# Identity products in TensorE's waits of the last batch's chain, and all input rows' products first at the end

## The chip, the cores and the metric

One core of a Trainium2 chip runs the whole program in one launch. The metric is the device time in microseconds; the kernel before was run three times.

## The reference

The inputs are `x` (4, 512, 256), the attention weights, a gate (256, 32) and the weights of 32 experts (96 inner columns each), all in float32. Cut to what matters:

```
qkv    = x @ w_qkv                                   # 16 heads of 16
scores = where(causal, (q / 4) @ k.T, -1e10)
a      = softmax(scores) @ v @ w_out
x      = layernorm(x + a)
w      = softmax(x @ gate); take the 4 largest of 32, scaled to sum 1
for each token and each of its 4 experts e:
    g, u = split(x @ gate_up[e]);  y_e = (u * silu(g)) @ down[e]
x      = layernorm(x + sum over the 4 experts of w_e * y_e)
```

There are 2048 tokens, so 8192 pairs of token and expert. The pairs are sorted by expert into tiles of 128 rows; each expert's last tile is filled up, and 95 tiles are computed.

## The kernel before, in words

**The plan.** `make_plan` writes one list of small units. Each engine walks this list and emits its own part of each unit, so each engine's instructions are in the order of the list, and an instruction that waits holds up all that is behind it on its engine. Semaphores join the engines. PSUM has eight banks of 512 float32 columns: banks 0 and 1 serve the row maxima ("max"), 2 and 3 the scores ("st"), 4 and 5 the products with v ("pv"), 6 and 7 in turn the many small units (the tuple `MISC`).

**The last batch's chain.** For the batch with number `B - 1` = 3 the list ends, after the last score and "pv" units, with: "norm" (transposes of the raw output, L612), "att" (transposes of the normalised one, L621), four "proj" (output projection and router logits, L660; VectorE adds the input and takes the statistics behind each, L1025 to L1034), "fix", "find" and "mark" (VectorE finds the four experts of each token, L1049 to L1074), "place" (TensorE sums the marks, so that each pair gets its row, L670), "slots", "count" (L677), "ends" (L684) and "table" (L708). From the table TensorE and SyncE read at which row each tile begins and which expert it belongs to. The semaphore `max_free` reaches `5 * PAIRS` = 160 once VectorE has read the last row maximum.

**Rows out to memory.** GpSimd scatters every token's row four times into `scratch_slots` (L1300), four batches of 16 scatters each. SyncE's queue holds, in this order: "early" (loads of the first `EARLY` = 17 tiles, L414, which only need the rows of batches 0 to 2), "fill" (32 stores of padding behind each expert's rows, L495), a wait for the padding and for all rows of batch 3 (L496 to L499), and the loads of the other 78 tiles (L414 again, called from L501).

**The experts.** TensorE works in a pipeline of four stages for each tile: transposes (L717), gate and up product (L730), transpose of the hidden rows (L740), down product (L746). This pipeline runs once over the tiles 0 to 16, is drained, and runs once over 17 to 94. ScalarE copies the result to `Y` (L899) and GpSimd scatters it into `scratch_y` (L1307).

**The end.** SyncE waits for all scatters and loads `YL`, sixteen transfers of 512 KB, two for each n of eight (L507). For each n TensorE adds in one bank, with the identity as the stationary operand: the input rows `X` (L778, one matmul) and two of the four experts' rows (L781, two matmuls). GpSimd adds the other two (L1314), VectorE joins both sums (L1229), takes the statistics (L931 to L936) and, for the n before, finishes the scale (`refine`, L941 to L949); ScalarE scales the rows (L803) and SyncE writes the result (L510). `X` is already normalised at that time (the wait on `ln_out`, L772). The kernel before uses bank n % 4, so from n = 4 on it waits for VectorE (L776).

Of the kernel before, what the change touches and what calls it, by code (L numbers as in the profile page):

```python
# [12 lines left out]
B, S, D = 4, 512, 256  # L13
H, HD = 16, 16
NE, FF = 32, 96
NT = B * S // 128
# [5 lines left out]
TILES = B * S * TOPK // 128 + NE - 1  # L22
# [10 lines left out]
PAIRS = 8 * B  # L33
# [144 lines left out]
def build(nc, x, w_qkv, w_out, gate, gup, dwn, out):  # L178
    ctx = ExitStack()
    with ctx:  # L180
# [9 lines left out]
        place = [base]  # L190
# [10 lines left out]
        X = sb("X", [128, NT, D], F32)  # L201
# [8 lines left out]
        idf = sb("idf", [128, 128], F32)  # L210
        idb = sb("idb", [128, 128], BF16)
# [70 lines left out]
        YL = at("YL", [128, NT // 2, 2, TOPK, D], F32)  # L282
        PS = ctx.enter_context(nc.psum_tensor("PS", [128, 8, 512], F32))
# [15 lines left out]
        for u in plan:  # L299
            kinds[u[0]] = kinds.get(u[0], 0) + 1  # L300
            rank[u] = kinds[u[0]]
            if u[0] in MISC:
                n_misc += 1
                k = n_misc % 2
# [16 lines left out]
        max_full, max_free = sem("max_full"), sem("max_free")  # L321
# [13 lines left out]
        gu_full, sg_out, hh_out = sem("gu_full"), sem("sg_out"), sem("hh_out")  # L335
        ht_full, ht_out = sem("ht_full"), sem("ht_out")
        y_full, y_out = sem("y_full"), sem("y_out")
        yk_out = [sem(f"yk_out{r}") for r in range(NY)]
        yl_in = [sem(f"yl_in{a}") for a in range(NT // 2)]
        late_sum, early_sum, x_sum = sem("late_sum"), sem("early_sum"), sem("x_sum")  # L340
# [171 lines left out]

        @block.tensor
        def _(e):
            for u in plan:
                kind, a = u[0], u[1:]
                if kind in MISC:
                    k = 6 + bank[u][0]
                    done = misc_full[bank[u][0]]
                if kind == "xt":  # L520
# [4 lines left out]
                    for q in range(4):  # L525
                        t = e.transpose(PS[:, k, 128 * q:128 * q + 128],
                                        X[:, 4 * b + q, 128 * c:128 * c + 128], idf[:, :])
                    t.then_inc(done, 1)
                elif kind == "qk":
# [3 lines left out]
                    for c in range(2):  # L533
                        e.wait_ge(*free(("xt", b, c)))
                        t = e.matmul(PS[:, k, :], WQ[:, c, 128 * m:128 * m + 128], XT[:, b % 2, c, :],  # L535
                                     start=(c == 0), stop=(c == 1))
                    t.then_inc(done, 1)
                elif kind == "v":
# [4 lines left out]
                    for q in range(2):  # L543
                        t0 = 128 * (2 * half + q)
                        for c in range(2):
                            t = e.matmul(PS[:, k, 256 * q:256 * q + 256], XT[:, b % 2, c, t0:t0 + 128],  # L546
                                         WQ[:, c, 512:768], start=(c == 0), stop=(c == 1))
                    t.then_inc(done, 1)
                elif kind == "max":
                    i, n = a  # L550
                    g, r = i // 4, (i // 4) % RG
# [5 lines left out]
                    for h, qt, c0 in pair_scores(n, 2 * (i % 4), 3, 2, 1):  # L557
                        w = 128 * (qt + 1)
                        e.matmul(PS[:, kk, c0:c0 + w], QS[r][0:96, h, 128 * qt:128 * qt + 128], KS[r][0:96, h, 0:w],  # L559
                                 start=(c0 == 0), stop=False, skip_group_check=True)  # L560
# [10 lines left out]
                elif kind == "st":  # L571
                    p, n = a
                    g, r = p // 4, (p // 4) % RG
# [16 lines left out]
                elif kind == "pv":  # L590
                    g, n = a
# [176 lines left out]
            load_experts(EARLY)  # L768
            experts(EARLY, TILES)

            e.wait_ge(hh_out, TILES)
            e.wait_ge(ln_out, NT)  # L772
            for n in range(NT // 2):
                k = n % 4
                if n >= 4:
                    e.wait_ge(x_sum, n - 3)  # L776
                sums = PS[:, k, :].rearrange("p (q d) -> p q d", q=2)
                e.matmul(sums, idf[:, :], X[:, 2 * n:2 * n + 2, :], start=True, stop=False)  # L778
                e.wait_ge(yl_in[n], 32)
                for r in range(2):  # L780
                    t = e.matmul(sums, idf[:, :], YL[:, n, :, r, :], start=False, stop=(r == 1))  # L781
                t.then_inc(early_sum, 1)

        @block.scalar
# [139 lines left out]
        def _(e):  # L924
# [300 lines left out]
            for t in range(0, NT + 2, 2):  # L1225
                if t < NT:
                    e.wait_ge(early_sum, t // 2 + 1)
                    e.wait_ge(late_sum, t // 2 + 1)
                    e.tensor_tensor(X[:, t:t + 2, :], PS[:, t // 2 % 4, :].rearrange("p (q d) -> p q d", q=2),  # L1229
                                    YL[:, t // 2, :, 2, :], ALU.add).then_inc(x_sum, 1)  # L1230
                    variance(t, x_sum, t // 2 + 1)
                if t:
                    refine(B + t // 2, t - 2, 2)
# [103 lines left out]
```

## Time and profile before

| | us |
|---|---|
| median of three runs | 473.64 |
| lowest and highest run | 470.53, 474.44 |
| time of the execution that was profiled | 470.53 |
| its span, first to last instruction | 468.8 |
| around the span (470.53 - 468.8) | 1.7 |
| PE busy | 401.1 (86%) |
| DVE, ACT, POOL busy | 281.8, 245.8, 244.0 |
| mean granted TensorE clock | 0.954 of full speed |

PE is TensorE, PEld its weight loads, DVE VectorE, ACT ScalarE, POOL GpSimd, SP SyncE (SPq its queue of issued transfers). All starts are in microseconds from the span's first instruction. PEclk is the TensorE clock that was granted, 1.00 being 2.4 GHz and 0.50 being 1.2 GHz. A float32 matmul stands in the records as two. In brackets behind a row is the idle time before it and what ended it.

### The profile page before, as it was taken

How to read it: one execution, taken by the hardware profiler on the slowest of the kernel's cores; microseconds unless marked ns; L12 is line 12 of the kernel's file. 1: busy time of each engine (PE TensorE's matmuls, PEld its weight loads, DVE VectorE, ACT ScalarE, POOL GpSimd, SP SyncE). 2: the span in 40 equal slices, each digit the busy share in tenths (PEclk: the TensorE clock that was granted, in tenths of full speed). 3: DMA queues.
4: the chain of work that ended last, by engine and by line, in shares of the span. 5: the costliest groups of instructions: out<-in, count | busy, mean ns of one | idle time of the engine just before them, and what ended most of it. 6: DMA issues, size and time to landing. Idle time of an engine off the chain costs nothing.

```text
span 468.8 us, 9779 instructions
## 1 busy us (share of the span) xinstructions
PE 401.1 (86%) x2613; PEld 268.1 (57%) x2613; DVE 281.8 (60%) x835; ACT 245.8 (52%) x594; POOL 244.0 (52%) x362
## 2 busy tenths in 40 slices
PE   5755899999988899978988717979999999996692
PEld 2422565455564356544544416859889998984240
DVE  1225774787459985899797394534555555551295
ACT  1412265676454676558757143544666666654054
POOL 4301242533332387635874737777777667765341
PEclk9989899999999999999999876998999999999697
DMA  4689473385467157497557249979755556300993
GB/s 161 148 173 174 125 130 88 92 147 100 108 186 143 27 105 163 131 215 193 172 157 212 93 138 300 286 229 307 205 162 176 155 169 171 110 3 4 395 383 116
DMA packets 55795, 76.77 MB, mean 164 GB/s; under 512 B 9650, under 2 KB 47804, under 8 KB 54208
## 3 DMA queue, kind: packets, MB, share of 16 engines
q1 hardware_dynamic: 48112, 59.22, 49.0%
q0 software_dynamic: 7632, 16.93, 10.1%
q8 instruction: 25, 0.41, 0.4%
q14 instruction: 26, 0.21, 0.2%
HBM read 46.23 MB, written 33.75 MB: 171 GB/s over the span
## 4 chain that ended last, share of the span: by engine, by line
PE 56%; DVE 17%; DMA 9%; SPq 6%; issue 6%; POOL 4%; ACT 1%; ACTq 0%; DVEq 0%; POOLq 0%
PE PS L730 11%; PE PS L746 7%; PE PS L602 6%; PE PS L535 6%; PE PS L559 5%; DVE MX L989 5%; PE PS L581 4%; PE PS L717 4%; SPq L495 3%; POOL scratch_slots L1300 2%; DMA scratch_qk<-PA 2%; PE PS L546 2%; PE PS L563 2%; PE PS L740 2%; PE PS L660 2%
## 5 line engine op out<-in xcount | busy, mean ns | idle before, releaser
L845 ACT ACTIVATE PT<-PS 128x512 f32<-128x512 f32 x160 | 92.9, 596 | 49.2 <-PE PS L581 44.2
L1307 POOL DMA_INDIRECT scratch_y<-Y,XG x95 | 93.6, 985 | 36.8 <-ACT Y L899 25.1
L989 DVE TENSOR_REDUCE MX<-PS 128x1 f32<-128x384 f32 (+1 forms) x192 | 88.5, 503 | 37.1 <-PE PS L563 37.0
L1283 POOL TENSOR_SCALAR_AFFINE_SELECT PT<-PT 128x256 f32<-128x256 f32 (+1 forms) x140 | 50.9, 372 | 75.9 <-ACT PT L845 74.0
L1300 POOL DMA_INDIRECT scratch_slots<-XP,RI x64 | 63.1, 986 | 35.9 <-DVE XP L1118 19.0
L730 PE MATMUL PS<-W,XGT 128*128 x380 | 80.5, 336 | 0.3 <-DVE XGT L1204 0.2
L559 PE MATMUL PS<-KS,QS 96*128 96x512 bf16 (+3 forms) x256 | 61.6, 303 | 21.1 <-DVE MX L989 12.5
L730 PEld LDWEIGHTS PS<-W,XGT 128*128 128x128 f32 x380 | 61.8, 196 | 1.0 <-issue 0.9
L581 PE MATMUL PS<-QS,KS 98*128 98x512 bf16 (+3 forms) x256 | 60.9, 299 | 1.4 <-ACT PT L845 1.4
L1211 DVE SCALAR_TENSOR_TENSOR HH<-PS,XG,SG 128x96 f32<-128x96 f32 x95 | 30.2, 318 | 52.5 <-ACT SG L887 52.0
L746 PE MATMUL PS<-W,HT 96*128 x190 | 57.3, 383 | 0.0
L1204 DVE COPY XGT<-PS 128x256 f32<-128x256 f32 x95 | 40.3, 425 | 20.4 <-PE PS L717 20.2
L559 PEld LDWEIGHTS PS<-KS,QS 96*128 96x128 bf16 x256 | 21.3, 100 | 51.0 <-DVE MX L989 28.2
L887 ACT ACTIVATE SG<-PS 128x96 f32<-128x96 f32 x95 | 23.9, 251 | 47.9 <-PE PS L730 47.9
L602 PE MATMUL PS<-PT,V 128*32 128x256 f32 (+3 forms) x512 | 44.0, 441 | 0.0
L899 ACT ACTIVATE Y<-PS 128x256 f32<-128x256 f32 x95 | 36.5, 384 | 13.7 <-PE PS L746 2.1
L1277 POOL TENSOR_TENSOR PA<-RE,PA 128x512 bf16<-128x512 f32 x16 | 18.5, 1156 | 47.7 <-ACT PA L832 47.6
L563 PE MATMUL PS<-mneg,idb 128*128 128x256 bf16 (+1 forms) x160 | 40.6, 253 | 0.0
L717 PE MATMUL PS<-idf,XG 128*128 128x128 f32 x190 | 37.5, 280 | 3.2 <-DMA XG<-scratch_slots 2.2
L535 PE MATMUL PS<-XT,WQ 128*128 128x512 f32 x64 | 35.3, 688 | 1.3 <-DMA WQ<-in_L_attn_w_qkv_dram 1.3
L717 PEld LDWEIGHTS PS<-idf,XG 128*128 128x128 f32 x190 | 27.3, 145 | 13.3 <-issue 4.1
L581 PEld LDWEIGHTS PS<-QS,KS 98*128 98x128 bf16 x256 | 24.5, 98 | 13.9 <-ACT PT L845 5.0
(169 smaller groups left out, 552.9 us busy)
## 6 DMA issues: line engine op xcount, KB each, us to landing
XG<-scratch_slots SPq DMA_DIRECT2D x95, 130.0 KB, 2.7
YL<-scratch_y SPq DMA_DIRECT2D x16, 512.0 KB, 10.7
scratch_qk<-PA SPq DMA_DIRECT2D x48, 128.0 KB
KS<-scratch_qk SPq DMA_DIRECT2D x48, 128.0 KB, 7.2
W<-_L_ffn_gate_up_proj_dram SPq DMA_DIRECT2D x16, 288.0 KB, 3.6
scratch_slots<-pad SPq DMA_DIRECT2D x33, 130.0 KB, 7.4
QS<-scratch_qk SPq DMA_DIRECT2D x8, 384.0 KB, 5.0
W<-in_L_ffn_down_proj_dram SPq DMA_DIRECT2D x8, 288.0 KB, 5.6
```

The costliest lines, as they stand in the source:

```text
L535: t = e.matmul(PS[:, k, :], WQ[:, c, 128 * m:128 * m + 128], XT[:, b % 2, c, :], start=(c == 0), stop=(c == 1))
L559: e.matmul(PS[:, kk, c0:c0 + w], QS[r][0:96, h, 128 * qt:128 * qt + 128], KS[r][0:96, h, 0:w], start=(c0 == 0), stop=False, skip_group_che ...
L581: t = e.matmul(PS[:, kk, c0:c0 + w], KS[r][0:98, h, 128 * j:128 * j + 128], QS[r][0:98, h, 128 * j:512], start=(c0 == 0), stop=True, skip_ ...
L602: t = e.matmul(PS[32 * h:32 * h + 32, 4 + r, 128 * j:512], V[b % 2][:, j, 4 * (g % 4) + h, :], PT[:, p % NPT, piece, c0:c0 + w], start=(j ...
L717: t = e.transpose(PS[:, j % 2, 128 * c:128 * c + 128], XG[:, j % NXG, 128 * c:128 * c + 128], idf[:, :])
L730: t = e.matmul(PS[:, 2 + j % 2, 0:2 * FF], XGT[:, j % 2, c, :], W[:, bass.ds(reg[j] + 2 * FF * c, 2 * FF)], start=(c == 0), stop=(c == 1))
L746: e.matmul(PS[:, 6 + j % 2, 0:D], HT[:, j % 2, :], W[0:FF, bass.ds(reg[j] + 4 * FF, D)], start=True, stop=True).then_inc(y_full, 1)
L845: e.activation(PT[:, p % NPT, n, :], PS[:, 2 + (rank[u] - 1) % 2, :], ACT.Exp).then_inc(st_exp, 1)
L989: t = e.tensor_reduce(M[:, h, qt:qt + 1], PS[:, kk, c0:c0 + w], AX.X, ALU.max)
L1283: e.affine_select(out=d, in_=d, compare_op=ALU.is_ge, fill=0.0, base=0, pattern=[[0, 1 if n < 2 else 2], [1, 128]], channel_multiplier=-1) ...
L1300: e.indirect_dma_start(out=XS[:, :], out_offset=bass.IndirectOffsetOnAxis(ap=RI[:, b % 2, TOPK * q + n:TOPK * q + n + 1], axis=0), in_=XP[ ...
L1307: e.indirect_dma_start(out=YK[:, :], out_offset=bass.IndirectOffsetOnAxis(ap=XG[:, j % NXG, D + 1:D + 2].bitcast(I32), axis=0), in_=Y[:, j ...
```

## The change

In the last batch's chain TensorE multiplies the identity (bf16, 128x128) with the identity repeated to 512 columns, into bank 0, ahead of six units: 3 times ahead of the last "norm", 4 ahead of the last "att", 3 ahead of the first "proj", 20 ahead of "place", 11 ahead of "ends" and 7 ahead of "table": 48 in all. Nothing reads the products. Each group stands behind a wait for `max_free`, as VectorE read bank 0 until then. At the end the products of all eight pairs of input rows come first, each n in bank n; the wait before them is for the last tile's `Y` (`y_out`) instead of its hidden rows (`hh_out`), since banks 6 and 7 are used too, and the waits for `x_sum` are gone.

```diff
+            def keep_busy(n):
+                for _ in range(n):
+                    e.matmul(PS[:, 0, :], idb[:, :], idb[:, :].unsqueeze(1).broadcast_to([128, 4, 128]), start=True,
+                             stop=True)
+
+            idle = {("norm", B - 1, 3): 3, ("att", B - 1, 1): 4, ("proj", B - 1, 0): 3, ("place", B - 1): 20,
+                    ("ends",): 11, ("table",): 7}
             for u in plan:
                 kind, a = u[0], u[1:]
+                if u in idle:
+                    e.wait_ge(max_free, 5 * PAIRS)
+                    keep_busy(idle[u])
...
-            e.wait_ge(hh_out, TILES)
+            e.wait_ge(y_out, TILES)
             e.wait_ge(ln_out, NT)
             for n in range(NT // 2):
-                k = n % 4
-                if n >= 4:
-                    e.wait_ge(x_sum, n - 3)
-                sums = PS[:, k, :].rearrange("p (q d) -> p q d", q=2)
-                e.matmul(sums, idf[:, :], X[:, 2 * n:2 * n + 2, :], start=True, stop=False)
+                e.matmul(PS[:, n, :].rearrange("p (q d) -> p q d", q=2), idf[:, :], X[:, 2 * n:2 * n + 2, :],
+                         start=True, stop=False)
+            for n in range(NT // 2):
                 e.wait_ge(yl_in[n], 32)
                 for r in range(2):
-                    t = e.matmul(sums, idf[:, :], YL[:, n, :, r, :], start=False, stop=(r == 1))
+                    t = e.matmul(PS[:, n, :].rearrange("p (q d) -> p q d", q=2), idf[:, :], YL[:, n, :, r, :],
+                                 start=False, stop=(r == 1))
                 t.then_inc(early_sum, 1)
...
-                    e.tensor_tensor(X[:, t:t + 2, :], PS[:, t // 2 % 4, :].rearrange("p (q d) -> p q d", q=2),
+                    e.tensor_tensor(X[:, t:t + 2, :], PS[:, t // 2, :].rearrange("p (q d) -> p q d", q=2),
```

## Rows read from the trace of the kernel before

**Rows 1.** Busy time by stretch: from:to, length, engines' busy us, clock, DMA share, GB/s
```profile
261.00:265.40 4.40, 2.01 (x11) 1.51 (x12) 0.69 (x2) 1.09 (x2) 3.23 (x5) 1.00 0.25 91
265.40:268.80 3.40, 3.40 (x8) 2.36 (x7) 1.75 (x7) 0.00 (x0) 2.81 (x4) 0.50 0.35 122
268.80:275.60 6.80, 1.66 (x7) 0.95 (x5) 6.23 (x31) 0.41 (x2) 3.27 (x5) 1.00 0.23 80
275.60:289.30 13.70, 6.86 (x51) 5.76 (x52) 8.37 (x43) 6.97 (x10) 7.03 (x9) 0.50 0.83 254
...
316.40:320.00 3.60, 3.60 (x16) 3.36 (x15) 1.39 (x4) 0.76 (x4) 2.82 (x3) 0.53 0.95 312
320.00:428.00 108.00, 107.76 (x680) 96.44 (x680) 55.59 (x150) 68.60 (x246) 76.42 (x79) 1.00 0.50 148
...
432.60:442.90 10.30, 5.62 (x7) 2.52 (x8) 1.70 (x6) 0.00 (x0) 2.53 (x2) 0.50 0.94 356
```

**Rows 2.** Timeline of PE, last batch's chain: start, length, line, tile, count, idle before
```profile
261.64 0.63 PE L612 MATMUL PS<-idf,RAW 128*128 128x128 f32 x4 [0.81 <-ACT RAW L852]
263.24 0.63 PE L621 MATMUL PS<-idf,AN 128*128 128x128 f32 x4 [0.97 <-DVE AN L1013]
264.65 5.81 PE L660 MATMUL PS<-WO,AT 128*128 128x288 f32 x16 [0.78 <-ACT AT L858]
275.98 0.18 PE L670 MATMUL PS<-MB,low 128*128 128x32 bf16 x1 [5.52 <-DVE MB L1074]
...
280.23 0.23 PE L684 MATMUL PS<-ui,NB 32*128 32x96 bf16 x1 [3.20 <-DVE NB L1130]
...
282.65 0.37 PE L708 MATMUL PS<-idf,TF 128*2 128x128 f32 x1 [2.15 <-DVE TF L1152]
283.95 1.08 PE L717 MATMUL PS<-idf,XG 128*128 128x128 f32 x4 [0.94 <-issue]
```

**Rows 3.** Timeline of PE in the attention: a bf16 matmul of 512 columns and the next
```profile
217.14 0.38 PE L559 MATMUL PS<-KS,QS 96*128 96x512 bf16 x1
217.36 0.22 PE L563 MATMUL PS<-mneg,idb 128*128 128x128 bf16 x1
```

**Rows 4.** Timeline of SyncE's queue: loads, padding, loads
```profile
275.77 9.84 SPq L414 DMA_DIRECT2D XG<-scratch_slots  x17
286.43 21.29 SPq L495 DMA_DIRECT2D scratch_slots<-pad  x32
312.23 26.61 SPq L414 DMA_DIRECT2D XG<-scratch_slots  x35
```

**Rows 5.** Chain that ended last: start, length, what
```profile
271.82 2.85 DMA scratch_slots<-XP,RI
...
307.38 3.87 DMA scratch_slots<-pad
```

**Rows 6.** Timeline of GpSimd: its last scatter of batch 3's rows
```profile
299.78 0.96 POOL L1300 DMA_INDIRECT scratch_slots<-XP,RI  x1 [0.31 <-issue]
```

**Rows 7.** Timeline of PE: the first tile after the 17 early ones
```profile
314.50 0.41 PE L717 MATMUL PS<-idf,XG 128*128 128x128 f32 x2 [2.05 <-DMA XG<-scratch_slots]
```

**Rows 8.** Timeline of PE at the end: the first and the last two experts' products
```profile
437.28 3.78 PE L781 MATMUL PS<-YL,idf 128*128 128x512 f32 x4 [7.87 <-DMA YL<-scratch_y]
...
458.19 1.88 PE L781 MATMUL PS<-YL,idf 128*128 128x512 f32 x4
```

**Rows 9.** Timeline of GpSimd at the end: its sums for n = 2 and n = 7
```profile
443.70 1.26 POOL L1314 TENSOR_TENSOR YL<-YL 128x512 f32<-128x512 f32 x1 [2.58 <-DMA YL<-scratch_y]
...
457.08 1.27 POOL L1314 TENSOR_TENSOR YL<-YL 128x512 f32<-128x512 f32 x1 [1.87 <-DMA YL<-scratch_y]
```

**Rows 10.** Timeline of VectorE at the end: one of the eight L936, and the last two joins L1229
```profile
446.45 1.11 DVE L936 TENSOR_SCALAR VE<-MV 128x2 f32<-128x2 f32 x1
...
458.94 0.69 DVE L1229 TENSOR_TENSOR X<-PS,YL 128x512 f32<-128x512 f32 x1
...
461.47 0.69 DVE L1229 TENSOR_TENSOR X<-PS,YL 128x512 f32<-128x512 f32 x1
```

## The prediction, made before the changed kernel was run

> **What bounds the kernel now.** I read the page's slices first, to see where PE is not busy and where the clock is low: the routing chain behind the attention, a short hole at 312 us, and the end. Then busy times by stretch [rows 1]: from 320 to 428 us PE is busy for 107.76 of 108 us at the higher clock. That is the experts' steady run; the change leaves it alone, and whatever moves its start moves the end. Three places are touched, each with another bound.
>
> First, the last batch's chain. The timeline of PE [rows 2] shows six idle times that end on ACT or DVE: 0.81, 0.97, 0.78, 5.52, 3.20 and 2.15 us. Their cost is not the idle time itself, which goes to other engines, but the clock: at 1.2 GHz (0.50) from 265.4 to 268.8 and from 275.6 to 289.3 us [rows 1].
>
> Second, the seam between the 17 early tiles and the rest. PE waits 2.05 us for a load and goes on at 314.50 [rows 7]. Who is late there? SyncE's queue [rows 4]: loads from 275.77, padding from 286.43, the late loads from 312.23. It starts when a scatter of batch 2, issued at 271.82, has landed, and between padding and late loads lies the landing of the last padding, 3.87 us [rows 5]. No part of this waits for TensorE's work on batch 3. This is the row that decides the forecast.
>
> Third, the end. GpSimd's sums run when their data has landed, the last at 457.08 [rows 9], which is the memory's pace. VectorE's last join runs at 461.47 [rows 10], 4.4 us behind its data. A backlog of that size comes from the start: the first two experts' products take 3.78 us at the low clock, the last two 1.88 [rows 8].
>
> **The change part by part.** *Identity products.* A bf16 matmul of 512 columns takes 0.22 us from start to start [rows 3], at half the clock 0.44 as an estimate. At the higher clock the groups take 3 x 0.22 = 0.66, 0.88, 0.66, 4.4, 2.42 and 1.54 us, each less than its idle time [rows 2]. So 48 matmuls, 10.6 us of PE, cost nothing; the cover is the wait for ACT or DVE. What stands behind each group on PE is the unit that waits anyway. The added wait (`max_free`) is long met: the row maxima end before the last scores. No DMA is added, and SyncE's and GpSimd's queues are passed by nothing.
>
> *What they give.* If the clock stays up, the projections lose half of 3.4 us [rows 1], 1.7, and the table comes 1.7 earlier. The early tiles start at about 282.2 instead of 283.95. Until 289.3 they ran 5.35 us at the low clock [rows 1, 2]; an all-PE stretch would save 2.7, but the pipeline's fill waits for copies, so I take 2.2 (bounds 1 and 2.7). The early tiles are done 3.9 us earlier.
>
> *Where that goes.* Into the wait at the seam: 2.05 becomes about 5.9 us, since the late loads stay at 312.23 [rows 4, 7]. What is late next is the same load. The gain that reaches the end is zero, plus or minus 0.5 for batch 3's scatters, which come 1.7 us earlier into a busy memory (0.83 to 0.95 of its share [rows 1]).
>
> *What it costs there.* PE has idled before every fall of the clock in this trace: before 275.6 it was busy for 1.66 of 6.8 us, at 432.6 nothing had run since 429.4. After 2.05 us of idle plus a slow fill it fell too, and tiles ran at 0.53 for 3.60 us [rows 1]. After 5.9 us of idle it will have fallen before the first late tile. The busy low stretches lasted 5.35 us at 283.95 and 5.6 at 437.28 [rows 1, 2, 8]; so I expect 5 us instead of 3.6, and at half speed each costs half: +0.7 us. Bounds: -1.8, if the clock stays up (all of 3.60 / 2), and +1.7, if it is low for another 3.4 us as from 265.4.
>
> *The end.* The eight input products are 8 x 2 records of 0.43 (1.88 for four, less 0.16 of drain at the last [rows 8]) = 6.9 us, now between about 429 (the steady run is over at 428, and the last `Y` is copied) and 436, where PE stood idle until 437.28. That keeps the clock up over the following 1.3 us. Each n then needs 1.7 us of PE instead of 2.6, less than the memory's pace (from 443.70 to 457.08 are five steps of 2.68 [rows 9]). Following n by n: first sum at 437.28 + 1.88 = 439.16; VectorE's own work for one n is 2.53 (461.47 - 458.94), so it keeps up with the data; its last join comes at 457.08 + 1.88 = 458.96, against 461.47 [rows 8, 9, 10]: -2.5. Against that: the outputs start earlier and one more of 256 KB goes out before the last load lands, at 356 GB/s [rows 1] 0.7 us; I charge 0.3. So -2.2. The waits for `x_sum` were met (no idle there), and `y_out` instead of `hh_out` costs 0.5 us of idle PE, with 1.3 to spare. Behind the last join nothing changes.
>
> At the end DVE and POOL meet. One L936, on 128x2 values, took 1.11 us [rows 10]: it ran from 446.45 to 447.56, and GpSimd's sum behind that of 443.70, a pace of 2.6 later, ran from about 446.3 for 1.26 us to the same end. After the change L936 begins about 3.6 us behind its data, which is inside the next sum of GpSimd again (2.6 to 3.9 behind the same data), but near its end, 0.2 us. If it falls at the beginning, once, the gain is 2.2 - 0.9 = 1.3. The Trainium skill, SBUF — State Buffer, "Who interferes with whom", says that a `tensor_scalar` on VectorE can need the port pair it shares with GpSimd and then blocks until the other is through; the trace agrees with its 1.11 us. The bounds of this part are 1.3 and 2.5.
>
> **Sum.** 0 (chain, swallowed at the seam) + 0.7 - 2.2 = -1.5 us. Against the profiled execution: 470.53 - 1.5 = 469.0. That execution is the fastest of three, 3.1 us under the median; I have no row that says where the others lost time, so I carry 3.1 over: 473.64 - 1.5 = **472.1**.
>
> **Rivals.** *A, the clock falls within the end.* Between the landings of n = 1 and n = 2 lie 3.84 us (1.26 busy and 2.58 idle on GpSimd [rows 9]); PE would be busy for 1.7 of them. Before 275.6 a thinner stretch let it fall, while from 261.0 to 265.4, with 2.01 of 4.40 busy, it was granted 1.00 and fell right behind [rows 1]. Then the end loses what it won but 0.5: 473.8. For it: the share, 1.7 / 3.84 = 44%, near that row's 46%. Against: the input products have just filled 7 us. 15%.
>
> *B, slower: the identity products overrun.* If the clock is low when they begin and they do not raise it, the 20 take 8.8 us in 5.5, the 11 take 4.8 in 3.2, the 7 take 3.1 in 2.15: 3.3 + 1.6 + 0.9 = 5.8 us late. The seam has 2.05 to give; 3.7 reach the late tiles. With the end's -2.2 that is +1.5, 475.1. The point from which it decides is an overrun of 2.05 + 2.2 = 4.3 us. Against: PE's work at the low clock from 283.95 and from 437.28 did bring the higher one back after some 5.5 us, and 20 products would be 8.8. Transposes stand between the first groups. By the Trainium skill, TensorE: Matmul & The Clock Gate, "Part 4: PE-mode transpose", transposes do not count as a busy PE in the same way, which would leave the first ten products to hold the clock alone and makes B likelier; no row here separates the two kinds. 10%.
>
> *C, faster: the gain passes the seam.* If batch 3's scatters and not the padding released the late loads, the 3.9 us would go through: 472.1 - 3.9 = 468.2. Against: the last scatter is issued at 299.78 [rows 6] and even with 2.85 us to land is 8 us ahead of the last padding's landing. 6%.
>
> *D, faster: the slower runs were slow by the clock.* Where PE stretches are short, whether the clock falls may differ from run to run, and two runs of three were over 3 us slower. If the change removes most of that, the median comes to 469.0 or less, say 468.6. For it: the two low stretches at 275.6 and 432.6 are gone. Against: the first was hidden at the seam in any case. 14%.
>
> That leaves 55% for the forecast.
>
> **Numbers.** 1% is 4.7 us: 468.9 and 478.4, about what a measurement of this kernel can tell from no change. Faster: C and D, 20%, with nothing for the forecast's own edge. Slower: half of B's worse forms, where its overrun also costs the early tiles, and unseen causes: 6%. Within: 74%. The range takes in C's side down to 468.0, and above A and most of B: 475.0; the bounds of the forecast itself (-1.8 - 0.5 - 2.5 = -4.8 and +1.7 + 0.5 - 1.3 = +0.9 on 473.64) are 468.8 and 474.5.
>
> **What would show it.** Clock 1.00 from 261 to the early tiles and no idle of PE over 2 us there; the mark matmuls ahead of "place" near 274.3; the early tiles done near 308.6; SyncE's first late load still near 312.2 and PE's wait before it near 6 us, then 0.50 for about 5 us; first join near 439.2 and last near 459.3 (shifted by the seam's cost), with clock 1.00 from 429. Wrong would be: a first late load that moves by over 1 us, a clock that stays up over the seam, a fall behind n = 1 at the end.

## The result, and the profile after

| | median of | us | lowest to highest |
|---|---|---|---|
| before | 4 | 473.28 | 470.53 to 474.44 |
| after | 4 | 467.37 | 466.82 to 467.92 |

The ratio is 0.9883, with its 95% interval 0.9838 to 0.9928: shorter by 5.9 us, where 1.5 was forecast, and 0.6 us below the range. Here and below the ratio compares fast runs alone (none more than 1.5% above the fastest of its series), while medians and means take in all runs. The profiled execution took 466.82 us (span 465.1, clock 0.978) against 470.53 (468.8, 0.954), so the profiles show only 3.7 us of it.

Busy time by stretch after (from:to, length, PE PEld DVE ACT POOL, clock, DMA share, GB/s), against [rows 1]:

```profile
259.40:280.70 21.30, 17.61 (x110) 9.32 (x106) 14.72 (x75) 7.83 (x11) 12.58 (x16) 1.00 0.41 129
280.70:307.20 26.50, 25.74 (x153) 21.61 (x153) 12.33 (x34) 13.39 (x50) 20.27 (x24) 1.00 0.96 297
...
313.00:318.30 5.30, 5.25 (x18) 4.29 (x19) 1.76 (x5) 0.74 (x3) 4.08 (x5) 0.50 0.92 277
...
435.40:456.70 21.30, 15.87 (x32) 5.42 (x32) 16.21 (x66) 8.31 (x24) 10.15 (x8) 1.00 1.03 405
```

The clock is 1.00 through the chain and the early tiles and again through the end's products. It is low in one place, around the seam, and there for longer than before: 5.3 us of busy PE, where it was 3.60.

The timeline of PE in the last batch's chain and at the seam (start, length, line, tile, count, idle before), against [rows 2, 7]; L518 are the identity products:

```profile
259.41 0.82 PE L518 MATMUL PS<-idb 128*128 128x512 bf16 x3
...
263.29 4.12 PE L671 MATMUL PS<-WO,AT 128*128 128x288 f32 x16
267.25 4.48 PE L518 MATMUL PS<-idb 128*128 128x512 bf16 x20
272.90 0.18 PE L681 MATMUL PS<-MB,low 128*128 128x32 bf16 x1 [1.18 <-DVE MB L1084]
...
277.16 0.20 PE L695 MATMUL PS<-ui,NB 32*128 32x96 bf16 x1 [0.79 <-DVE NB L1140]
...
279.49 0.27 PE L719 MATMUL PS<-idf,TF 128*2 128x128 f32 x1 [0.50 <-DVE TF L1162]
280.68 0.63 PE L728 MATMUL PS<-idf,XG 128*128 128x128 f32 x4 [0.92 <-issue]
...
313.00 1.34 PE L728 MATMUL PS<-idf,XG 128*128 128x128 f32 x4 [5.77 <-DMA XG<-scratch_slots]
```

Behind each filler the consumer still waits for VectorE, now for 1.18, 0.79 and 0.50 us instead of 5.52, 3.20 and 2.15: the products fit. The projections take 4.12 us instead of 5.81. The early tiles run from 280.68 and then PE stands idle for 5.77 us: the gain lies in that bracket. What is late there is seen in SyncE's queue, against [rows 4]:

```profile
274.30 9.74 SPq L414 DMA_DIRECT2D XG<-scratch_slots  x17
284.71 22.09 SPq L495 DMA_DIRECT2D scratch_slots<-pad  x32
310.73 87.72 SPq L414 DMA_DIRECT2D XG<-scratch_slots  x78
431.61 8.63 SPq L507 DMA_DIRECT2D YL<-scratch_y  x16
445.19 16.66 SPq L510 DMA_DIRECT2D out_dram<-X  x8
```

From the first early load to the first late one are 36.43 us, before 36.46. The whole queue only stands 1.5 us earlier, from its first row on; the attention ends earlier too, ahead of anything that was changed. The end, on PE, VectorE (L1239) and GpSimd (L1324), against [rows 8 to 10]:

```profile
428.24 7.13 PE L785 MATMUL PS<-X,idf 128*128 128x512 f32 x16 [0.47 <-ACT Y L909]
436.42 1.98 PE L790 MATMUL PS<-YL,idf 128*128 128x512 f32 x4 [1.04 <-DMA YL<-scratch_y]
438.44 0.69 DVE L1239 TENSOR_TENSOR X<-PS,YL 128x512 f32<-128x512 f32 x1 [12.35 <-PE PS L790]
454.74 1.27 POOL L1324 TENSOR_TENSOR YL<-YL 128x512 f32<-128x512 f32 x1 [1.26 <-DMA YL<-scratch_y]
456.74 0.69 DVE L1239 TENSOR_TENSOR X<-PS,YL 128x512 f32<-128x512 f32 x1
```

The first pair takes 1.98 us instead of 3.78, and the last join stands 2.00 us behind GpSimd's last sum instead of 4.39. Then something new ends last. These are the instructions of L180, the program's closing line, after (engine's queue, operation, count, duration in ns min/median/max, first and last start):

```profile
L180 POOLq EVENT_SEMAPHORE  x2: 17/17/17, 464.9 to 465.0; - x2
L180 POOLq DRAIN  x1: 10138/10138/10138, 454.7 to 454.7; - x1
L180 SPq DRAIN  x1: 7/7/7, 463.8 to 463.8; - x1
```

and before:

```profile
L180 POOLq DRAIN  x1: 10132/10132/10132, 457.0 to 457.0; - x1
L180 SPq DRAIN  x1: 7/7/7, 468.5 to 468.5; - x1
```

GpSimd's closing drain (the instruction with which the engine ends the program) lasts 10.13 us from the start of its last sum. Before, it was over at 467.1 and SyncE, with the outputs, was last at 468.5. After, SyncE is through at 463.8 and waits until 464.9 for GpSimd.

The 3.7 us are, leg by leg between milestones of the two profiles:

| leg | before | after | difference |
|---|---|---|---|
| start to first early load | 275.77 | 274.30 | -1.5 |
| to first late load | 36.46 | 36.43 | 0.0 |
| to first `YL` load | 120.18 | 120.88 | +0.7 |
| to last join | 29.06 | 25.13 | -3.9 |
| to the span's end | 7.33 | 8.36 | +1.0 |

The first leg lies ahead of everything that was changed. The other four sum to -2.2.

### The profile page after: what moved, and what is told of

The parts are those of the page before. It is cut to its first block, busy times and chain, and to the rows that moved or that the text cites. A ratio compares the mean times of both kernels' runs of the same rounds, so it can differ in the third digit from the quotient of the medians.

```text
span 465.1 us, 9875 instructions
## 1 busy us (share of the span) xinstructions
PE 406.6 (87%) x2661; PEld 267.4 (57%) x2661; DVE 279.8 (60%) x835; ACT 245.4 (53%) x594; POOL 243.6 (52%) x362
## 4 chain that ended last, share of the span: by engine, by line
PE 58%; DVE 15%; DMA 10%; SPq 8%; issue 5%; ACT 2%; POOL 1%; ACTq 0%; DVEq 0%
PE PS L741 11%; PE PS L613 7%; PE PS L757 7%; PE PS L570 5%; PE PS L546 5%; DVE MX L999 5%; PE PS L592 4%; PE PS L728 4%; DMA YL<-scratch_y 3%; SPq L495 3%; PE PS L557 2%; DMA scratch_qk<-PA 2%; PE PS L574 2%; PE PS L671 2%; PE PS L751 2%
## 5 line engine op out<-in xcount | busy, mean ns | idle before, releaser
L741 PE MATMUL PS<-W,XGT 128*128 x380 | 79.4, 333 | 0.4 <-DVE XGT L1214 0.4
L909 ACT ACTIVATE Y<-PS 128x256 f32<-128x256 f32 x95 | 36.4, 383 | 13.5 <-PE PS L757 1.9
L1287 POOL TENSOR_TENSOR PA<-RE,PA 128x512 bf16<-128x512 f32 x16 | 18.5, 1156 | 46.4 <-ACT PA L842 46.3
L546 PE MATMUL PS<-XT,WQ 128*128 128x512 f32 x64 | 33.6, 658 | 1.5 <-DMA WQ<-in_L_attn_w_qkv_dram 1.5
```

The source lines that it names most:

```text
L741: t = e.matmul(PS[:, 2 + j % 2, 0:2 * FF], XGT[:, j % 2, c, :], W[:, bass.ds(reg[j] + 2 * FF * c, 2 * FF)], start=(c == 0), stop=(c == 1))
```

## The experiments

All kernels compute the whole reference. The chips differ: in three comparisons the kernel before takes about 517 us, in two others 470.4 and 471.0, near the first one's profile. I call them the 517 chips (two chips) and the 470 chips (two more), and compare times only within a kind. Distances from the first `YL` load on look alike on both kinds, and are compared across them.

### Each part alone (517 chips)

"Same" is the kernel before, unchanged. "Chain only" is the first part of the diff alone, "end only" the rest alone. "Clock only" keeps the end's old order and banks and gives TensorE work in the gap ahead of the first loads:

```diff
                 e.matmul(sums, idf[:, :], X[:, 2 * n:2 * n + 2, :], start=True, stop=False)
+                if n == 0:
+                    e.wait_ge(y_out, TILES)
+                    keep_busy(32, 4)
                 e.wait_ge(yl_in[n], 32)
```

> The kernel before, unchanged, run again as its own control. Theory 1 (the clock and the order in which the end's data lands differ from run to run): ratio 1.00 within 0.3%, but its own runs spread over 3 to 4 us, and in this profile the last join (L1229) lies at another distance behind the last issue of YL than 461.47 - 432.41 = 29.06 us. Theory 2 (before is steady, and the rest of the measured difference lies ahead of the last batch's chain): spread under 1 us and that distance 29.1 again.

> Identity products in the last batch's chain only; the end as before. My theory (the gain is swallowed by SyncE's queue): the early tiles end about 3.9 us earlier against the first load after the attention, SyncE's first late load stays 36.4 us behind its first early one, PE waits about 6 us for it, then the clock is at 0.50 for about 5 us; time 0.5 to 1 us longer than before. Rival (the chain carries a part of the 5.9 us): 1.5 to 4 us shorter than before.

> The new end only: input rows' products first, each in its bank; no identity products in the chain. My theory (all of the gain is the end's): 4 to 6.5 us shorter than before, ratio 0.987 or a little less than the full change, as the seam stays short; from the first YL issue to the last join 25 us instead of 29. Rival (half and half): about 2 to 3 us shorter.

> Before's order at the end, with 32 identity products into bank 4 behind the first input product, so that PE is busy until the first YL lands (bank 4 is free once the last Y is copied; the wait for that is added). If the clock alone makes the end's gain: the same as the new end only, -4 us or more. If the order (less PE work per n once data has landed) makes it: PE needs 2.6 us per n against a memory pace of 2.56, so VectorE's last join comes some 1 to 1.5 us later than with the new order; time 2 to 3 us shorter than before.

Measured: medians 520.94 for the same kernel again (before 517.31, ratio 0.9936 [0.9872, 1.0]), chain only 515.66 (1.000 [0.9965, 1.0036]), end only 514.57 (0.9961 [0.9919, 1.0002]), clock only 516.23 (0.9968 [0.9928, 1.0007]). The medians of single series say little where one kernel against itself differs by 3.6 us; the profiles say more. The end in clock only, timelines of SyncE, PE and VectorE:

```profile
484.15 8.28 SPq L507 DMA_DIRECT2D YL<-scratch_y  x16
...
480.55 7.07 PE L518 MATMUL PS<-idb 128*128 128x512 bf16 x32
489.09 1.98 PE L790 MATMUL PS<-YL,idf 128*128 128x512 f32 x4 [1.47 <-DMA YL<-scratch_y]
...
509.13 0.69 DVE L1238 TENSOR_TENSOR X<-PS,YL 128x512 f32<-128x512 f32 x1
```

The last join starts 24.98 us behind the first `YL` load, where end only has 24.70, and 2.11 us behind GpSimd's last sum, where the new order has 2.00. So the clock alone brings all but 0.1 us of what the end gains behind its data, with the old order and the old banks. Two expectations were missed: the end alone was to be 4 to 6.5 us shorter, and the kernel before, run again, was to spread over 3 to 4 us; it spread over 15.5 (510.21 to 525.73). Its last join comes 29.05 us behind the first `YL` load, as before. From the first early load to the first late one it takes 46.4 to 55.4 us on these chips, not 36.4.

### The same again, and the seam filled (517 chips)

The seam is filled by waiting for the last early tile's transposed rows and then 24 identity products; the rest is the kernel after:

```diff
             experts(0, EARLY)
+            e.wait_ge(xgt_out, EARLY)
+            keep_busy(24)
             e.wait_ge(tile_at, 3)
```

> The changed kernel itself, beside the kernel before on this chip, to have all four on one chip. Ratio 0.987 to 0.992 wherever the chip's memory is as quick as in the first profiles. In the trace: last join 25.1 us behind the first YL issue, and the end of the span 8.3 us behind the last join, since GpSimd's drain (10.1 us from its last sum) is the last thing to finish; the seam costs 0.5 to 1 us.

> Identity products in the chain only. If SyncE's queue swallows their gain: 0 to 1 us longer than before, and the first late load 36.4 us behind the first early one. If the chain carries part of the 5.9 us: 1.5 to 3 us shorter.

> The new end only. If the end carries all: 3 to 4 us shorter than before (4 us at the last join, less 1 us by which GpSimd's drain is then the last to finish), 0.5 to 1 us shorter than the full change. If half: 1.5 to 2.5 us.

> The changed kernel and 24 more identity products (5.2 us) at the seam, behind the last early tile and ahead of the wait for the first late load. If the low clock behind the seam is what the chain's early finish costs: clock 1.00 through the seam, 1.5 to 2.7 us shorter than the changed kernel. Rival (the stretch behind the seam waits for loads anyway): under 0.5 us.

Measured (before 516.95): after 515.03 (0.997 [0.9906, 1.0034]), chain only 515.51 (0.9999 [0.9943, 1.0054]), end only 514.69 (0.9968 [0.9913, 1.0022]), seam filled 515.06 (0.9992 [0.995, 1.0034]). The timelines of chain only,

```profile
475.21 8.29 SPq L507 DMA_DIRECT2D YL<-scratch_y  x16
...
480.21 3.78 PE L792 MATMUL PS<-YL,idf 128*128 128x512 f32 x4 [7.71 <-DMA YL<-scratch_y]
...
503.18 0.69 DVE L1240 TENSOR_TENSOR X<-PS,YL 128x512 f32<-128x512 f32 x1
```

and of end only,

```profile
475.81 8.17 SPq L507 DMA_DIRECT2D YL<-scratch_y  x16
...
500.51 0.69 DVE L1236 TENSOR_TENSOR X<-PS,YL 128x512 f32<-128x512 f32 x1
```

give the join at 27.97 and 24.70 us behind the first `YL` load: -3.3, with nearly the same pace of landings (GpSimd's last sum starts 22.93 and 22.71 us behind that load; behind that sum the join stands 5.04 and 1.99, so -3.05). The seam could not be tested here: the early tiles run on into the late ones with no more than 0.7 (seam filled) or 0.9 us (after) of idle PE, and that behind VectorE, not a load, so there was nothing to fill.

### The closing drain (517 chips)

To start GpSimd's drain earlier, VectorE takes the sum of n = 7:

```diff
+                if t == NT - 2:
+                    e.wait_ge(yl_in[t // 2], 32)
+                    e.tensor_tensor(YL[:, t // 2, :, 2, :], YL[:, t // 2, :, 2, :], YL[:, t // 2, :, 3, :],
+                                    ALU.add).then_inc(dve_step, step.one())
+                    e.wait_ge(dve_step, step.n)
...
-                    e.wait_ge(late_sum, t // 2 + 1)
+                    e.wait_ge(late_sum, min(t // 2 + 1, NT // 2 - 1))
...
-            for n in range(NT // 2):
+            for n in range(NT // 2 - 1):
```

The last kernel has this and the filled seam.

> The kernel before as its own control, for a further profile of its chain and seam. Theory (slow runs of before are those with long stretches at 1.2 GHz and a late batch-3 chain): ratio 1.00, time and mean granted clock of its single runs anticorrelated (-0.7 or stronger), spread 4 us or more.

> The changed kernel again, now in five rounds. If it takes away before's long low-clock stretches: its single runs spread less than before's, mean clock 0.95 or more, mean time 2.5 to 5 us shorter. If the profile's 3.7 us was luck of one execution: under 1.5 us.

> The changed kernel, with GpSimd's last sum (n = 7) made by VectorE ahead of its last join. If GpSimd's drain of 10.1 us behind its last sum sets the end of the changed kernel: from last join to the end 7.3 us instead of 8.3, last join 0 to 0.7 us later, so 0.3 to 1 us shorter. If the drain is covered by the last output: the end moves 0.7 us later.

> As the one with GpSimd's last sum on VectorE, with 24 identity products at the seam. Where PE waits at the seam (quick memory, as in the first profiles): clock 1.00 behind the seam and 1.5 to 2.7 us shorter than without them. Where the early tiles run into the late ones with no idle PE (as in the profiles of the last two calls): 0, or up to 2 us longer, as the products then delay the first late tile.

Measured (before 517.57): same 520.81 (1.0035 [0.9986, 1.0084]), after 514.26 (0.9977 [0.9943, 1.001]), VectorE's last sum 514.98 (0.9953 [0.9909, 0.9997]), with the seam 517.22 (1.0013 [0.9972, 1.0054]). The time behind the last join is 7.34 and 7.32 us with VectorE's sum and 8.31 to 8.39 in the kernels with the new end and GpSimd's; but the join itself comes 25.88 and 25.50 us behind the first `YL` load instead of 24.9. One microsecond is bought with 0.6 to 1.0. The kernel with the 24 products at the seam as well is 2.9 ± 1.1 us longer in the mean than the one without them, more than the 2 us that were expected at most; with GpSimd's sum the same products cost nothing clear (515.28 against after's 514.64). The difference is not explained.

The profile of the same kernel has a row that the first one lacks, in SyncE's waits (line waited for: us, times, longest):

```profile
SPq L399 <- DVE FI L1102: 4.0, 1, 4.0
```

and in its timelines of SyncE and VectorE:

```profile
282.81 9.52 SPq L414 DMA_DIRECT2D XG<-scratch_slots  x17
296.93 33.45 SPq L495 DMA_DIRECT2D scratch_slots<-pad  x32
...
296.26 0.16 DVE L1102 CAST FI<-BASE 1x32 int32<-1x32 f32 x1
```

`FI` holds the rows at which padding is stored, and it comes out of the chain. Here the first padding waits for it, 4.6 us behind the early loads' end, where [rows 4] show 0.8. When the chain ends that late, a faster chain can bring the late loads forward. Four of the twelve profiles on these chips have this wait, at 3.7 to 7.6 us: three of the five without products in the chain, and one of the seven with them. The lateness itself is older than the products: in these four the last transposes of "norm" start at 277.3 to 278.8 us, in the other eight by 275.1. What the products do behind that is seen at the projections: 5.58 to 7.07 us in all five profiles without them, 4.12 in six of the seven with them and 4.58 in one. Pooled over all series on these chips, with the standard error of the mean:

| kernel | executions | mean, us | over 518 us |
|---|---|---|---|
| before, same | 124 | 518.33 ± 0.37 | 48% |
| chain only | 22 | 515.47 ± 0.43 | 9% |
| end only | 22 | 514.88 ± 0.84 | 27% |
| after | 22 | 514.64 ± 0.59 | 9% |
| clock only | 12 | 516.83 ± 1.35 | 42% |
| seam filled | 10 | 515.28 ± 0.47 | 10% |
| VectorE's last sum | 12 | 514.75 ± 0.75 | 17% |
| with the seam | 12 | 517.62 ± 0.75 | 33% |

By these means each part alone is worth about 3 us on the 517 chips and both together 3.7 ± 0.7. The ratios don't show the chain's part: for chain only they are 1.000 and 0.9999. Its mean is shorter because it has few long executions, not because its short ones are shorter, so how much the chain's products give here stays open. That a part can come through the padding is shown in kind by the rows above, not in size. The control's own time and clock were expected to go together with -0.7 or stronger; in its twelve executions the correlation is -0.48, in all 124 it is -0.78.

### The chain in halves, and lengthened (470 chip)

"First ten" has the products ahead of "norm", "att" and "proj" alone, "last 38" those ahead of "place", "ends" and "table":

```diff
-            idle = {("norm", B - 1, 3): 3, ("att", B - 1, 1): 4, ("proj", B - 1, 0): 3, ("place", B - 1): 20,
-                    ("ends",): 11, ("table",): 7}
+            idle = {("norm", B - 1, 3): 3, ("att", B - 1, 1): 4, ("proj", B - 1, 0): 3}      # first ten
+            idle = {("place", B - 1): 20, ("ends",): 11, ("table",): 7}                      # last 38
```

"Chain later" is the kernel before with a comparison in the last "mark" done seven times instead of once:

```diff
+                    for _ in range(7 if b == B - 1 else 1):
                         e.tensor_tensor(OH[:, :, :], iot[:, :].unsqueeze(1).broadcast_to([128, 16, NE]),
                                         IE[:, :].unsqueeze(2).broadcast_to([128, 16, NE]),
                                         ALU.is_equal).then_inc(dve_step, step.one())
```

> Only the first ten identity products (before norm, att and proj). If the chain's length up to the padding's position (last RAW to FI) is what counts: last RAW to place 13.3 us as with all 48, and the mean time 2 to 3 us under before, as with all 48. If the early tiles' clock counts: under 1 us.

> Only the last 38 (before place, ends and table). If the chain's length counts: last RAW to place 15 to 16.3 us as before, and the mean within 1 us of before. If the early tiles' clock counts: early tiles at clock 1.00, and the mean 2 us or more under before.

> The kernel before with six repeats of a VectorE comparison (0.73 us each) in the chain, which make it 4.4 us longer. If SyncE's queue hides the chain altogether (my forecast): mean time within 1 us of before. If it hides only what lies before the queue reaches the padding: fast executions 1 to 3 us longer, those in which the padding already waits for the chain 4.4 us, mean 2 to 4.4 us longer.

> Control. Ratio 1.00. In its profile, if the first padding is issued later than 1 us behind the last of the 17 early loads, then FI is written right before it (within 0.7 us) and last RAW to place is 15 to 16.4 us.

Measured (before 470.40, of 35 executions): first ten 470.26 (0.998 [0.9945, 1.0016]), last 38 470.38 (1.0031 [0.999, 1.0073]), chain later 470.87 (0.9995 [0.9952, 1.0038]), same 470.54 (0.9976 [0.9932, 1.0019]). Neither half of the products changes the mean clearly (-0.2 ± 0.6 and +0.1 ± 0.6 us), and 4.4 us more of VectorE's work in the chain cost 0.7 ± 0.8 us of it. All 48 without the new end were not run on a 470 chip. The timelines of PE and SyncE of "chain later" show where the added time goes:

```profile
282.06 0.18 PE L670 MATMUL PS<-MB,low 128*128 128x32 bf16 x1 [9.86 <-DVE MB L1075]
...
319.56 0.86 PE L717 MATMUL PS<-idf,XG 128*128 128x128 f32 x4 [0.28 <-issue]
...
278.80 9.52 SPq L414 DMA_DIRECT2D XG<-scratch_slots  x17
288.90 21.73 SPq L495 DMA_DIRECT2D scratch_slots<-pad  x32
314.94 90.02 SPq L414 DMA_DIRECT2D XG<-scratch_slots  x78
```

PE's wait is 9.86 us instead of 5.52, the early tiles end later, and the whole idle time at the seam is gone (0.28). SyncE's queue goes its own way: 36.14 us from early to late loads. The seam's idle time is the chain's slack, and it was used up from the other side. What is more than the slack comes through: from the first late to the first `YL` load this profile has 122.5 us, where the others on the 470 chips have 119.3 to 120.9.

The same kernel again, timeline of PE:

```profile
266.31 4.12 PE L660 MATMUL PS<-WO,AT 128*128 128x288 f32 x16 [0.78 <-ACT AT L858]
...
316.87 0.66 PE L717 MATMUL PS<-idf,XG 128*128 128x128 f32 x2 [4.63 <-DMA XG<-scratch_slots]
```

The projections ran at the higher clock without any product in front, where in [rows 2] the same code took 5.81 us. They took 4.12 in "last 38" and "chain later" too, also without a product ahead of them. So in three of the four such profiles on 470 chips there was nothing to win at the projections, and the expectation for "last 38", a chain of 15 us or more up to "place", was missed (12.6). The seam's idle time of 4.63 us, too, is there without any product.

The halves keep the old end. "Last 38", timelines of SyncE, GpSimd and VectorE:

```profile
434.23 8.23 SPq L507 DMA_DIRECT2D YL<-scratch_y  x16
...
457.09 1.27 POOL L1324 TENSOR_TENSOR YL<-YL 128x512 f32<-128x512 f32 x1 [1.26 <-DMA YL<-scratch_y]
...
461.49 0.69 DVE L1239 TENSOR_TENSOR X<-PS,YL 128x512 f32<-128x512 f32 x1
```

GpSimd's last sum starts 22.86 us behind the first load and the last join 4.40 behind that, 27.26 in all ("first ten": 22.88 + 4.56). The kernel before has 24.67 + 4.39. Its data lands later: its sum for n = 2 starts 3.84 us behind that for n = 1 and the last 3.14 behind the one before, where the other steps are 2.56. This holds for all five profiles in which TensorE's instructions are those of before (before, its three repetitions and "chain later": 24.66 to 24.77 us to the last sum, join at 29.05 to 29.16) and for none of the other fifteen. In the same five, and in no other within 25 us of the first `YL` load, a packet of an instruction queue passes, 8 to 9 us behind that load. The view of the DMA queues of before from 440.41 to 441.41 us (queue and kind: packets, MB, share of 16 engines) has it:

```profile
q8 instruction: 1, 0.02, 6.9%
```

6.9% of 16 engines over 1.00 us is 1.1 us of one engine, and n = 2 is late by 1.3. So a load of instructions in the midst of the data is the likely cause of the late landings, and every change to TensorE's code moved it away. No run moved the packet alone, and why n = 7 is late again is open. Open too is why the halves' means show nothing of a join that came 1.6 to 1.8 us sooner in their profiles.

### The best version (another 470 chip)

After, and after with the filled seam and VectorE's last sum, edits as above.

> The changed kernel over five rounds. If its effect is the end alone (3.3 us at the last join, less 1.0 for GpSimd's drain, less 0 to 1 at the seam): 1.5 to 3 us under before, in mean and median. If the first comparison's 5.9 us was the effect: 5 us or more.

> The changed kernel with 24 identity products at the seam and GpSimd's last sum on VectorE. On a chip where PE waits at the seam: clock 1.00 behind it and 1.5 to 2.5 us under the changed kernel, and 0 to 0.5 more from the drain. If early tiles run into the late ones without idle PE: no gain, or 1 to 2 us longer.

Measured (before 471.01): after 468.81 (0.9978 [0.9935, 1.0022]), the version with both edits **466.61** (0.9934 [0.9891, 0.9977]), the fastest here. The seam of after, timeline of PE and busy time by stretch:

```profile
315.79 0.41 PE L728 MATMUL PS<-idf,XG 128*128 128x128 f32 x2 [3.38 <-DMA XG<-scratch_slots]
...
315.80:324.00 8.20, 7.66 (x39) 6.86 (x40) 3.58 (x10) 2.25 (x9) 6.07 (x8) 0.79 0.96 300
```

and with the seam filled, the same two views, and then the closing line and VectorE:

```profile
309.55 5.34 PE L518 MATMUL PS<-idb 128*128 128x512 bf16 x24
314.73 0.38 PE L728 MATMUL PS<-idf,XG 128*128 128x128 f32 x2
315.42 0.41 PE L728 MATMUL PS<-idf,XG 128*128 128x128 f32 x2 [0.30 <-DMA XG<-scratch_slots]
...
314.70:324.00 9.30, 8.99 (x56) 7.65 (x55) 4.79 (x14) 3.83 (x15) 7.17 (x8) 1.00 0.97 298
...
L180 POOLq DRAIN  x1: 10135/10135/10135, 451.5 to 451.5; - x1
...
456.11 0.68 DVE L1240 TENSOR_TENSOR YL<-YL 128x512 f32<-128x512 f32 x1
```

The clock over the late tiles' start is 1.00 instead of 0.79, and from the first late load to the first `YL` load it takes 119.29 us instead of 120.17: a low clock at the seam costs 0.9 in this pair, and is avoidable. The drain starts at 451.5 and is over before SyncE; VectorE's sum ahead of the join takes most of that back. By the profiles the version gains 0.9 + 0.2 us on after; the means differ by 2.0 ± 0.9 (466.43 against 468.42).

Pooled over both 470 chips: before and same 470.66 ± 0.31 (68 executions, standard deviation 2.6, from 464.1 to 476.1); after 2.2 ± 0.7 us less, the last version 4.2 ± 0.7 less. The interval of the ratio includes 1 for after, and does not for the last version.

## Why the prediction was wrong in the number and right in most steps

**The level: this step failed.** "I have no row that says where the others lost time, so I carry 3.1 over." The range was laid around the median of three, 473.64, as if what made two of three executions longer had to be in the changed kernel too. It was not: all four of after took 466.8 to 467.9, close to the profiled one. Over 68 executions on the 470 chips the kernel before has a median of 470.7 and a standard deviation of 2.6; drawing four of these gives a median of 473.28 or more in 3 draws of 100. Its time goes with the granted clock (correlation -0.72). So the profiled execution, which I called the fastest and corrected for, was the typical one, and 470.5 less the forecast 1.5 is 469.0; after has a mean of 468.4 in its later twelve. The 5.9 us of the first comparison are likewise too large. In means they are 5.5: 2.2 are repeated, 2.2 are the first four of before above the 68, and 1.1 the first four of after below its later twelve. Four drawn from the 68 against four from those twelve differ by 5.9 or more in 2 draws of 100. Whether those first executions were off by the draw or by their chip stays open.

**The chain, forecast 0: right where it could be seen on the 470 chips.** The clock stayed up (1.00 from 259.4), the table came 1.7 us earlier behind the first early load, as forecast, the early tiles were done 5.2 us sooner (307.23 against 312.45), 3.7 of it beyond the queue's own 1.5 (forecast 3.9), and SyncE's early-to-late distance did not move (36.46, 36.43). The sign "a first late load that moves by over 1 us" did show, at 1.5, but the first early load had moved as far, ahead of the change. Halves of the change gave -0.2 and +0.1 us of the mean, a longer chain +0.7; the whole chain alone was not run there. On the 517 chips the mean with the chain alone is 2.9 us shorter and the ratio is 1.00, so there it is open. Rival C asked whether batch 3's scatters release the late loads; the link I did not see is the padding's index `FI`, which is read from the chain ahead of the first padding. The trace of before has it ready at 278.56, 7.9 us ahead of the first padding; I had not looked at how much room that was, and on another chip an execution uses it up.

**The seam's clock, forecast +0.7: right in this pair.** It is +0.70 between the two profiles, with 5.77 us of idle and 5.3 us at 0.50 as forecast (5.9 and 5), and 0.9 was given back when it was filled. But it is no constant cost of the change: another profile of before has 4.63 us of idle and 120.94 us for this leg, and another of after 3.38 and 120.17.

**The end, forecast -2.2: too small, -3.9; the landings failed, not the clock.** Of the -2.5 for the clock, less a charge of 0.3, the clock's part was right: behind GpSimd's last sum the last join moved from 4.39 to 2.00 us (-2.4), and at steady landings the old end has 4.40, 4.56 and 5.04 (last 38, first ten, chain only) against 2.00, so -2.4 to -3.0. "Its last join comes at 457.08 + 1.88" was right to 0.1. What failed is that it took 457.08 as the memory's pace and so put a change of the landings at nothing. The "five steps of 2.68" are four of 2.56 and one of 3.14, and the step ahead of them is 3.84. In after these late steps are gone, and the last sum starts 23.13 us behind the first `YL` load instead of 24.67: -1.5. That they go with an instruction packet among the loads is shown by coincidence in twenty profiles, not by a run. The charge of +0.3 for contention has no row. VectorE's L936, weighed there at up to 0.9, took 0.17 us at most places and once 0.48; before has a second long one, 0.78 us at 457.60, that the forecast left out.

**The closing drain, not in the forecast: +1.0.** "Behind the last join nothing changes" was wrong: behind it stands GpSimd's drain, 10.13 us long in every profile, with 1.4 us of room before (467.1 against 468.5) and none after. I had read the last row of each engine's work and not the closing line.

**Sum.** 0 + 0.7 - 3.9 + 1.0 = -2.2 by the profiles' legs behind the first, where 0 + 0.7 - 2.2 = -1.5 was forecast and the repetition has 2.2 ± 0.7 less. That the forecast of the difference came so near is partly luck: an error of -1.7 at the end and one of +1.0 behind it. At equal landings the change is worth only 0.7 - 2.4 + 1.0 = -0.7 to 0.7 - 3.0 + 1.0 = -1.3 us. The order of the products and the eight banks add 0.1 us to the clock's part by the clock-only kernel's profile.

**Rivals.** A (a fall within the end): the clock was 1.00 from 435.4 to 456.7, wrong; but the gap of 3.84 us that it was built on did not occur in after either, where the longest step is 2.98. B (overrun): the 20 took 4.48 us of a wait of 5.5, wrong. By the rule on transposes that B names (the Trainium skill, TensorE: Matmul & The Clock Gate, "Part 4: PE-mode transpose"), the first ten products alone had to hold the clock. It was held, but in three of four profiles on 470 chips it was held without these products too, so these runs don't decide it. D (the longer executions were longer by the clock) has its correlation, which is no proof of a cause. On the 517 chips 48% of the executions of the kernel before were over 518 us, and 9 to 33% of those of the kernels with products in the chain; on the 470 chips neither half of them moved the mean, and after's standard deviation over twelve, 2.0 us, is not much less than 2.6.

## What to carry to other kernels

Before a median of three is used as a level, ask how far the executions of one kernel lie apart; a row that explains the profiled execution is worth more than an offset that no row explains. Work given to a waiting TensorE pays where its next busy work is what ends last: it bought 2.4 to 3.0 us at the end and, on the 470 chips, nothing clear in a chain with slack behind it, and the longer wait that it left there had to be filled in turn. When an end is shortened, read the closing line of every engine for what comes last next. And before an average of landings is called the memory's pace, look at the single steps and at what else the queues carried there.

## What the runs showed of the hardware that I had not expected

- GpSimd's closing drain takes 10.13 us from the start of its last instruction, in the old end, the new one, and when it starts 3 us earlier (10.132, 10.138, 10.135).
- One program takes 470 us on some chips and 517 on others. Where it takes longer, engines stand idle inside the attention and the early tiles for something that the profile can't name, as here on ScalarE in the same kernel's timeline:

```profile
269.03 0.60 ACT L852 ACTIVATE RAW<-PS 128x512 f32<-128x512 f32 x1 [8.00 <-remote]
```

- The clock's falls are not a property of the code alone: the same projections behind the same waits, without products ahead, took 4.12 us in three executions and 5.81 in another on the 470 chips, and 5.58 to 7.07 in five on the 517 chips.
- When a kernel's own instructions are loaded may show in how its data lands: in the five profiles with an instruction packet (0.02 MB) 8 to 9 us behind the first `YL` load, the load for n = 2 landed 1.2 to 1.3 us late and the last one 0.5 to 0.8; in none of the fifteen others was n = 2 late. TensorE's instructions were those of before in just these five. The cause is likely, not tested. It is worth some 1.5 us of the first comparison's -3.9 at the end.
